# Scan: six of sixteen raw products by VectorE in steps of 256 columns, and softplus by Tanh in the input loop

## The reference, cut to what matters

```python
dt = jnp.clip(jax.nn.softplus(jnp.einsum('blo,eo->ble', dt_raw, W_dt) + b_dt), 0.0001, 10.0)
A = -jnp.exp(jnp.minimum(A_log, 5.0))

def step(h, inp):
    dt_t, B_t, C_t, u_t = inp
    dA = jnp.exp(jnp.clip(dt_t[:, :, None] * A, -20.0, 0.0))
    dB_u = jnp.clip(dt_t[:, :, None] * B_t[:, None, :] * u_t[:, :, None], -10.0, 10.0)
    h = jnp.clip(h * dA + dB_u, -100.0, 100.0)
    y = jnp.einsum('bdn,bn->bd', h, C_t)
    return (h, y)
```

## Time and profile before

| | |
|---|---|
| median of 3 runs | 1869.72 us (1868.13 to 1870.24) |
| the profiled execution, its own time | 1870.31 us |
| the profiled execution, span from first to last instruction | 1868.5 us |
| PE busy | 1580.0 us, 85% of the span |
| VectorE busy | 1353.5 us, 72% |
| ScalarE busy | 1034.3 us, 55% |
| GpSimd busy | 521.2 us, 28% |
| input loop, softplus | 1034.0 to 1148.5 us, 1149.0 to 1175.5 us of the span |
| first products of the scan | 1175.5 to 1189.06 us |
| positions 1 to 31 of the scan | 1189.06 to 1542.8 us |

### The profile page before, as it was taken

The page is one execution under the profiler, slowest core; times in us unless marked ns, Lnnn a source line. Parts: engine busy times, 40 slices in busy tenths (PEclk is TensorE's granted clock), DMA queues, the critical chain, the costliest instruction groups (busy, mean ns, idle before and its releaser), DMA issues. The chain is left out here.

```text
span 1868.5 us, 36875 instructions
## 1 busy us (share of the span) xinstructions
PE 1580.0 (85%) x10997; PEld 1031.1 (55%) x11024; DVE 1353.5 (72%) x3801; ACT 1034.3 (55%) x2779; POOL 521.2 (28%) x559
## 2 busy tenths in 40 slices
PE   5999999999998999799895885477777774999999
PEld 2666666666665455466563674366655563444444
DVE  4777777777777666577686444799999996677765
ACT  2666666666665333344332225899999992322321
POOL 1211111111111100000000721688888880322200
PEclk9999999999999999899897898798988886999999
DMA  5011011011010900000366000000000001000000
GB/s 136 24 34 34 23 34 34 23 34 34 23 34 5 349 8 0 1 1 1 97 212 183 0 0 0 1 1 0 0 0 0 0 0 51 1 7 6 12 6 17
DMA packets 69336, 66.48 MB, mean 36 GB/s; under 512 B 5695, under 2 KB 66834, under 8 KB 69266
## 3 DMA queue, kind: packets, MB, share of 16 engines
q1 hardware_dynamic: 66598, 64.00, 11.5%
q10 hardware_dynamic: 2668, 1.62, 0.3%
HBM read 61.41 MB, written 4.19 MB: 35 GB/s over the span
## 5 line engine op out<-in xcount | busy, mean ns | idle before, releaser
L1995 PE MATMUL ss_y_ps<-ss_h,ss_diag 128*128 128x256 f32 x1024 | 264.4, 422 | 133.8 <-ACT sc_dt L1913 93.2
L1995 PEld LDWEIGHTS ss_y_ps<-ss_h,ss_diag 128*128 128x128 f32 x1024 | 215.6, 214 | 182.4 <-issue 79.1
L595 ACT ACTIVATE x_probs<-x_probs,x_neg_max 128x257 f32<-128x257 f32 x512 | 253.5, 498 | 63.2 <-DVE x_neg_max L696 63.2
L696 DVE CUSTOM_DVE_ANT_0 x_probs<-x_s_ps,x_mask_b 128x257 f32<-128x257 f32 x512 | 187.3, 423 | 133.5 <-PE x_s_ps L403 133.5
L1897 ACT ACTIVATE ss_decay<-sc_dt,sc_a 128x256 f32 (+1 forms) x496 | 207.8, 479 | 1.8 <-DVE ss_h L1960 1.8
L1951 DVE SCALAR_TENSOR_TENSOR ss_decay<-ss_decay,ss_h 128x1024 f32<-128x1024 f32 x124 | 152.3, 1228 | 27.7 <-ACT ss_decay L1897 27.4
L1907 ACT ACTIVATE ss_come<-ss_dtu,sc_xd 128x256 f32<-128x256 f32 x384 | 163.6, 512 | 6.6 <-POOL ss_dtu L1853 6.6
L413 PE MATMUL x_pT_ps<-all_ident,x_probs 128*128 128x128 f32 x1024 | 162.4, 282 | 0.6 <-DVE x_pT L703 0.6
L1867 POOL TENSOR_TENSOR ss_diag<-all_ident,sc_xd 128x512 f32<-128x512 f32 x128 | 158.8, 1240 | 12.8 <-PE ss_y_ps L1995 2.9
L703 DVE COPY x_pT<-x_pT_ps 128x512 f32<-128x512 f32 x256 | 161.3, 668 | 0.5 <-PE x_pT_ps L413 0.5
L1960 DVE CUSTOM_DVE_ANT_0 ss_h<-ss_come,ss_decay 128x1024 f32<-128x1024 f32 x124 | 149.9, 1209 | 0.0
(11 more groups left out here) (373 smaller groups left out, 3072.0 us busy)
## 6 DMA issues: line engine op xcount, KB each, us to landing
x_ctx_t<-ctxT SPq DMA_DIRECT2D x48, 514.0 KB, 3.8
kept_ctx_t<-ctxT SPq DMA_DIRECT2D x16, 514.0 KB, 8.2
kept_ctx_n<-ctx SPq DMA_DIRECT2D x16, 512.0 KB, 8.5
x_ctx_n<-ctx SPq DMA_DIRECT2D x16, 512.0 KB, 4.1
all_x<-x SPq DMA_DIRECT2D x4, 512.0 KB, 7.8
x_mid<-all_x SPq DMA_DIRECT2D x32, 64.0 KB, 4.0
all_x<-x_mid SPq DMA_DIRECT2D x4, 512.0 KB, 7.6
out<-all_x SPq DMA_DIRECT2D x8, 256.0 KB, 2.0
```

What stands on the lines that cost most here:

```text
L595: ins = nc.scalar.activation(probs[p][:, n, :], probs[p][:, n, :], ACT.Exp, scale=-1.0, bias=neg_max[p][:, n:n + 1], accum_out=sums[p][:, ...
L696: vec.tensor_tensor_reduce(probs[p][:, n, :], s_ps[:, c, 0:S2], mask_b[:, :], -1.0, -MASKED, ALU.add, ALU.min, neg_max[p][:, n:n + 1]).the ...
L1995: ins = nc.tensor.matmul(y_ps[p][:, 0:DI], diag[q][:, m, :], h[q][:, m, :], start=(q == 0 and m == 0), stop=(q == NQ - 1 and m == NH - 1))
```

## The change

`OWN` goes from (0, 0, 0, 4) to (0, 0, 2, 4): ScalarE makes ten raw products per position where it made twelve, VectorE six where it made four. VectorE makes each by its own tensor_scalar of 256 columns that multiplies by a number per partition and clips at 10, where it made four by one tensor_tensor. `mine` is now called twice a position, for group 2 behind `state` 3 and for group 3 behind `state` 0.

Softplus(x) = max(x, 0) + ln(1 + exp(-|x|)) is computed as max(x, 0) - ln(0.5 + 0.5 tanh(|x|/2)). Tanh is taken in the input loop, one position at a time, and Ln of four quarters follows behind the loop; both Exp of the quarters are gone. The clip of `dt` moves in front of softplus, into the loop, with its limits turned into limits of the raw value.

```diff
--- before.py
+++ after.py
@@ -1594,12 +1594,13 @@
 XW = 1 + 2 * NS
 NH = 4
 NQ = NS // NH
-OWN = (0, 0, 0, 4)
+OWN = (0, 0, 2, 4)
 BY_ACT = [q for q in range(NQ) if OWN[q] < NH]
 BY_DVE = [q for q in range(NQ) if OWN[q] > 0]
 RING = 3
 TINY = float(np.exp(-20.0))
 LN_Q = 4
+DT_LOW, DT_HIGH = float(np.log(np.expm1(1e-4))), float(np.log(np.expm1(10.0)))
 
 
 def stage_scan1(nc, g):
@@ -1637,6 +1638,7 @@
         u = [sb(f"u{p}", [P, 2 * DI]) for p in range(2)]
         uT = [sb(f"uT{p}", [P, DI]) for p in range(2)]
         soft = sb("soft", [P, T, DI])
+        half = sb("half", [P, 1])
 
         x_ps, c_ps, u_ps, d_ps = (ps(n, [P, BANK]) for n in ("x_ps", "c_ps", "u_ps", "d_ps"))
         c_ps = [c_ps, ps("c_ps1", [P, BANK])]
@@ -1646,7 +1648,7 @@
         xn_ready, xT_psum, xT_sb, conv_psum, u_sb = (sem(n) for n in ("xn_ready", "xT_psum", "xT_sb", "conv_psum", "u_sb"))
         uz_sb, uT_psum, uT_sb, xd_psum, xd_sb, dt_sb = (sem(n) for n in ("uz_sb", "uT_psum", "uT_sb", "xd_psum", "xd_sb", "dt_sb"))
         waited_pool = sem("waited_pool")
-        waited, abs_sb, exp_sb, ln_sb, soft_sb, clip_sb = (sem(n) for n in ("waited", "abs_sb", "exp_sb", "ln_sb", "soft_sb", "clip_sb"))
+        waited, abs_sb, tanh_sb, ln_sb, soft_sb, raw_sb = (sem(n) for n in ("waited", "abs_sb", "tanh_sb", "ln_sb", "soft_sb", "raw_sb"))
         block = ctx.enter_context(nc.Block())
         a_step = sem("a_step")
         W_LOADS = 8
@@ -1693,7 +1695,7 @@
                         ins = mm(d_ps[:, 0:XW], uT[(p + 1) % 2][:, c * P:(c + 1) * P], w_x[:, c, :], start=(c == 0), stop=(c == DB - 1))
                     ins.then_inc(xd_psum, 1)
 
-            pe.wait_ge(prep, TAPS + 2 + 9)
+            pe.wait_ge(prep, TAPS + 3 + 9)
             pipeline(pe, step, 2, 1, TAPS)
 
         @block.scalar
@@ -1710,6 +1712,10 @@
                     act.wait_ge(dt_sb, t - 1)
                     act.sem_inc(waited, 1)
                     nc.scalar.activation(soft[:, t - 2, :], dt[:, t - 2, :], ACT.Abs).then_inc(abs_sb, 1)
+                if inside(t - 3):
+                    act.wait_ge(abs_sb, t - 2)
+                    act.sem_inc(waited, 1)
+                    nc.scalar.activation(soft[:, t - 3, :], soft[:, t - 3, :], ACT.Tanh, scale=0.5).then_inc(tanh_sb, 1)
 
             nc.scalar.dma_start(w_in_T[:, :], g.dram["L1_attn_W_in_T"]).then_inc(w_in, 16)
             nc.scalar.dma_start(taps[:, :, :].rearrange("p k e -> p (k e)"),
@@ -1721,20 +1727,14 @@
             nc.scalar.dma_start(a[:, :], g.dram["L1_attn_A_log"].rearrange("(a n) -> a n", a=1).to_broadcast([P, NS])).then_inc(w_in, 16)
             nc.scalar.dma_start(rowmask[:, :], g.dram["c_rowmask"]).then_inc(w_in, 16)
             norm_coefficients(nc, g, act, None, ln_step, lnw)
-            pipeline(act, step, 2, 2, TAPS)
-
-            act.wait_ge(abs_sb, T)
+            pipeline(act, step, 2, 3, TAPS)
+
+            for q in range(LN_Q):
+                t = slice(q * LT, (q + 1) * LT)
+                act.wait_ge(tanh_sb, (q + 1) * LT)
+                nc.scalar.activation(soft[:, t, :], soft[:, t, :], ACT.Ln, scale=0.5, bias=half[:, :]).then_inc(ln_sb, 1)
             act.wait_ge(a_step, 1)
             nc.scalar.activation(a[:, :], a[:, :], ACT.Exp).then_inc(a_step, 1)
-            for half in range(2):
-                quarters = range(half * LN_Q // 2, (half + 1) * LN_Q // 2)
-                for q in quarters:
-                    s = slice(q * LT, (q + 1) * LT)
-                    nc.scalar.activation(soft[:, s, :], soft[:, s, :], ACT.Exp, scale=-1.0).then_inc(exp_sb, 1)
-                for q in quarters:
-                    s = slice(q * LT, (q + 1) * LT)
-                    act.wait_ge(exp_sb, q + 1)
-                    nc.scalar.activation(soft[:, s, :], soft[:, s, :], ACT.Ln, bias=1.0).then_inc(ln_sb, 1)
 
         @block.gpsimd
         def _(pool):
@@ -1783,28 +1783,29 @@
                     vec.tensor_copy(xd[:, t - 1, :], d_ps[:, 0:XW]).then_inc(xd_sb, 1)
                     dve.wait_ge(xd_sb, t)
                     vec.scalar_tensor_tensor(dt[:, t - 1, :], w_dt[:, :], xd[:, t - 1, 0:1], b_dt[:, :],
-                                             ALU.mult, ALU.add).then_inc(dt_sb, 1)
+                                             ALU.mult, ALU.add).then_inc(raw_sb, 1)
+                    dve.wait_ge(raw_sb, t)
+                    vec.tensor_scalar(dt[:, t - 1, :], dt[:, t - 1, :], DT_LOW, DT_HIGH, ALU.max, ALU.min).then_inc(dt_sb, 1)
 
             arrived_stats(nc, g, dve, x_in, stats)
             norm_coefficients(nc, g, None, dve, ln_step, lnw)
             vec.memset(ones[:, :], 1.0).then_inc(prep, 1)
             vec.memset(cb[:, :], 0.0).then_inc(prep, 1)
+            vec.memset(half[:, :], 0.5).then_inc(prep, 1)
             dve.wait_ge(w_in, 16 * W_LOADS)
             for k in range(TAPS):
                 vec.tensor_tensor(w_c[:, k, :], w_in_T[:, 0:DI], taps[:, k, :], ALU.mult).then_inc(prep, 1)
             vec.tensor_scalar(a[:, :], a[:, :], 5.0, None, ALU.min).then_inc(a_step, 1)
-            dve.wait_ge(prep, 2)
-            split_row(vec, dve, prep, TAPS + 2, cb3[:, :], rowmask, (c_hi[:, :], c_rest[:, :], c_f[:, :]), cb[0:3, :])
+            dve.wait_ge(prep, 3)
+            split_row(vec, dve, prep, TAPS + 3, cb3[:, :], rowmask, (c_hi[:, :], c_rest[:, :], c_f[:, :]), cb[0:3, :])
             pipeline(dve, step, 3, 1, TAPS)
             for q in range(LN_Q):
                 s = slice(q * LT, (q + 1) * LT)
                 dve.wait_ge(ln_sb, q + 1)
-                vec.scalar_tensor_tensor(dt[:, s, :], dt[:, s, :], 0.0, soft[:, s, :], ALU.max, ALU.add).then_inc(soft_sb, 1)
-                dve.wait_ge(soft_sb, q + 1)
-                vec.tensor_scalar(dt[:, s, :], dt[:, s, :], 1e-4, 10.0, ALU.max, ALU.min).then_inc(clip_sb, 1)
+                vec.scalar_tensor_tensor(dt[:, s, :], dt[:, s, :], 0.0, soft[:, s, :], ALU.max, ALU.subtract).then_inc(soft_sb, 1)
             dve.wait_ge(a_step, 2)
             vec.tensor_scalar(a[:, :], a[:, :], -1.0, None, ALU.mult).then_inc(a_step, 1)
-            dve.wait_ge(clip_sb, LN_Q)
+            dve.wait_ge(soft_sb, LN_Q)
 
 
 def scan_states(nc, g, uz, dt, xd, a):
@@ -1937,10 +1938,11 @@
                 dve.wait_ge(dtu_sb, t + 1)
                 if not (isinstance(t, int) and t < 2):
                     dve.wait_ge(h_sb, (t - 2) * NQ + q + 1)
-                m = OWN[q]
-                weight = xd[:, t, 1 + q * NH:1 + q * NH + m]
-                vec.tensor_tensor(come[q][k % 2][:, 0:m, :], dtu[k % 2][:, :].unsqueeze(1).to_broadcast([P, m, DI]),
-                                  weight.unsqueeze(2).to_broadcast([P, m, DI]), ALU.mult).then_inc(mine_sb, 1)
+                for m in range(OWN[q]):
+                    s = 1 + q * NH + m
+                    ins = vec.tensor_scalar(come[q][k % 2][:, m, :], dtu[k % 2][:, :], xd[:, t, s:s + 1], 10.0,
+                                            ALU.mult, ALU.min)
+                ins.then_inc(mine_sb, 1)
 
             def kept(t, k, q):
```

## The result

The changed kernel takes 1943.66 us (median of four runs, 1942.67 to 1946.61) against 1869.98 us (four runs, 1868.13 to 1872.53) for the kernel before: a ratio of 1.0396, 95% interval 1.0378 to 1.0414. That is slower by 73.7 us, or 4%. The forecast was 1905 us, slower by 35, with a range from 1850 to 1945. In the experiments two executions fell into a slow state, one of the kernel before (3822.61 us) and one of the six products in two instructions (1954.86 us), and the ratios leave them out.

What follows compares the result with a forecast made beforehand. VectorE, taking turns with GpSimd, was to bound the scan at 13.2 us per position. 1870.3 - 15.1 (softplus, first products, table load) + 50.8 (scan) = 1906.0, by the median 1905 us; range 1850 to 1945.

Steps and rivals of the forecast that it cites:

- The bound and its change of hands: Scan: ScalarE sets the pace before the change, VectorE after it, with positions of 12 to 14.4 us.
- GpSimd was to be busy for longer per instruction: Scan: a sign listed for the prediction being right, GpSimd busy for longer per instruction; no size given.
- the ties: Scan: whether GpSimd gets in after every step or every second, called undecided; worth 2.4 us per position.
- The step alone: Scan, VectorE: a 256-column tensor_scalar takes 0.348 us alone, 0.26 from start to start; six take 1.56 us.
- The turns: Scan: steps and GpSimd take turns at SBUF, up to 0.89 us each; turns changing hands, 60 in 100.
- The size of the turns: Scan: six steps cost 2.9 to 5.3 us per position, middle 4.1, adding 50.8 us in all.
- the dear corner: Scan: GpSimd gets in after each step; two steps cost 1.4 us, four 3.9, adding 86.8 us in all.
- Softplus and the first products: Before the scan: softplus saves 12.2 us, fewer first products 1.6 and a table load 1.3, together 15.1 us.
- The input loop at nothing: Input loop: added Tanh and clip hidden behind waits for TensorE, costing nothing; without cover 29 us at most.
- Loads at each Tanh: Input loop: possible table loads for Tanh, for which the range reached up to 1945 us; no chance given.
- VectorE keeping its turn through a group: Scan rival: each group waits once, 2.5 us of steps, position 11.5 us, total 1856 us; 14 in 100.
- turns not fought over: Scan rival: GpSimd waits when steps come, total 1831 us, or steps leave it alone, 1854; 12 in 100.

Runs made afterwards that it cites:

- Who asks first: Changed kernel with its six steps multiplying by a constant 0.25 instead of a number per partition, compared there with other runs' traces; 1880.33 us.

## Why the prediction was right or wrong

*The bound and its change of hands: right.* VectorE sets the scan's pace, with positions of 14.44 us, `kept` does not wait for `decays`, and ScalarE has gaps that `state` ends, as the prediction listed under what would show it. One of its signs failed: GpSimd was to be busy for longer per instruction, and `diagonals` went from 1.24 us in the mean, as the page of before has it, to 1.04, since the ties fell to GpSimd.

```profile
L1867 POOL TENSOR_TENSOR ss_diag<-all_ident,sc_xd 128x512 f32<-128x512 f32 x128 | 158.8, 1240 | 12.8 <-PE ss_y_ps L1995 2.9
```

*The step alone: right.* 0.348 us and 0.26 apart were worked out from the earlier trace rows; the shortest step takes 0.340, and four undisturbed ones 1.13 us.

*The turns: right as a mechanism.* Each disturbed step waits for one GpSimd instruction. Long instructions on the same columns, another place for the steps, PSUM as their source, or a shorter `bound` each take most of the loss away, so what is paid for is the turns lost, and not the columns.

*The size of the turns: wrong, and this is the step that failed.* It is the term "together 2.9 to 5.3 us; I take the middle, 4.1, since nothing decides the ties". Measured are 1.48 + 3.91 = 5.39 us, the dear corner (1.4 + 3.9) in both groups. The 1.29 us too few per position are 38.7 us in thirty positions, and the forecast missed by 38.7 (the scan took 443.4 us for the 404.5 of the forecast). Something did decide the ties, and the prediction held a row for it: in the earlier trace rows a VectorE instruction with a number per partition started 0.03 us ahead of GpSimd and went second, and the step's lead was reckoned at "those same 0.03 us". The trace of after gives the step 0.01 us, less than the lead that had lost, and less than the 0.042 us that lost in other traces (under *Who asks first*). The run with a constant in place of that number shows the other end: there the pair goes through. And a loop that repeats itself does not draw lots: the six steps last 0.43, 1.20, 1.01, 0.81, 1.20 and 1.20 us, the same to 0.02 us, in each of the 24 positions from 1190.46 to 1522.55. So a middle between the corners was a time that the kernel had little way of taking. By the nearest row the sum was 1870.3 - 15.1 + 86.8 - 0.6 = 1941.4, against 1943.66.

*Softplus and the first products: right.* Forecast 15.1 us, measured 15.0 from the loop's first Silu on; the rest of the 16.2 is the earlier start of the loop. Counted so, `a` is 11.9 us earlier (forecast 12.2), and the wait, the clip and Tanh push the load behind the loop back by 1.25 us (116.73 us behind the first Silu instead of 115.48), where 0.95 were forecast. The first products and the load give 3.0 us (forecast 2.9).

*The input loop at nothing: right.* Silu's line loads a table once in the whole loop, and Tanh's 32 instructions of 0.42 us are hidden: the last Silu starts 111.25 us behind the first, for 111.26 before.

```profile
L1707 ACT ACT_TABLE_LOAD x1 | 1.3, 1283 | 0.0
```

*The rivals.* Loads at each Tanh fall with that row. VectorE keeping its turn through a group, and turns not fought over, fall with the 945 ns. Both happen elsewhere, though: the first in pairs without a number per partition, the second with the steps that GpSimd waits for, at 1857 us.

Open is why a number per partition costs a VectorE instruction its lead. The traces show that it does, by how much, and that such a step lasts 0.06 us longer; what the engine does in that time they do not show. It is not the computing of the number's address in the loop: the last of those instructions of VectorE starts at 1524.0 in the trace of after, and the positions behind that lose the same turns.

## What to carry to other kernels

Where VectorE and GpSimd both work from SBUF without pause, a new VectorE instruction is priced by the turns that it can lose to GpSimd, and only then by its columns: keep few long ones, put short ones where GpSimd waits for them anyway, or let them read from PSUM. Where two engines meet at the same place in every turn of a loop, as they do here, a tie falls the same way every time, so take the corner that the nearest row points to, and give the other corner a chance of its own instead of a middle.

## What the runs showed of the hardware that was not expected

Six short instructions cost from 2.4 to 5.4 us per position, by their place and one operand alone. The start in the trace does not by itself say who goes first: with a number per partition a lead of 0.01 us was not enough and one of 0.05 was, and without one 0.01 us was enough. By the Trainium skill (SBUF — State Buffer, "SBUF: two separate sides") the one that starts first gets the ports; taken as the start that the trace shows, the runs agree with it for steps without such a number and decide against it for a lead of 0.01 us with one. Tanh works from the table that Silu has loaded, where Sigmoid and Silu load one for each change.
